# A GNN layer's block loop: the GRU job one step earlier, TensorE's block sums one step earlier, ScalarE's dense gates one step later

## What is computed

```
h = relu(layernorm(x))                              # x: 12500 nodes x 128
att = sigmoid(h[src] @ Wa[:128] + h[dst] @ Wa[128:] + b_att)   # 400000 edges
messages = (h[src] @ W_msg + b_msg) * att
agg = segment_sum(messages, dst)                    # real destinations: see below
r, z = sigmoid(gi_r + gh_r), sigmoid(gi_z + gh_z)   # gi = agg @ W_ih.T + b_ih
n = tanh(gi_n + r * gh_n)                           # gh = h @ W_hh.T + b_hh
out = x + batchnorm_over_nodes((1 - z) * n + z * h) * gamma + beta
```

## Time and profile before

| | |
|---|---|
| median of 3 runs | 2257.42 us (2254.52 to 2258.43) |
| the profiled execution | 2257.88 us |
| its span, first to last instruction | 2256.1 us |
| busy: PE, DVE, ACT, POOL | 91%, 89%, 88%, 74% |
| mean granted TensorE clock | 0.965 of full speed |

### The profile page before, as it was taken

One profiled execution on the slowest core, in us unless ns is written; L12 is line 12 of the kernel. 1 busy time (PEld: TensorE's weight loads), 2 busy tenths in 40 slices (PEclk: granted clock), 3 DMA queues, 4 the chain that ended last, 5 costly groups with the idle time before them and its releaser, 6 DMA issues.

```text
span 2256.1 us, 53903 instructions
## 1 busy us (share of the span) xinstructions
PE 2055.7 (91%) x18202; PEld 1994.3 (88%) x18202; DVE 2012.9 (89%) x4413; ACT 1996.3 (88%) x6980; POOL 1660.4 (74%) x1578
## 2 busy tenths in 40 slices
PE   3536999999999999999999999999999999999997
PEld 3525999999999999999999999999999999999996
DVE  5967899999999999999999999999999999999974
ACT  1368999999999999999999999999999999999943
POOL 4575777777777777777777777777777777777760
PEclk8865999999999999999999999999999999999998
DMA  6862222222222222222222222222222222222236
GB/s 164 237 172 62 56 60 62 59 60 60 62 62 62 63 58 64 61 63 59 63 59 62 59 61 60 63 60 62 60 61 63 59 62 60 61 61 64 58 108 231
DMA packets 167473, 171.57 MB, mean 76 GB/s; under 512 B 79462, under 2 KB 131736, under 8 KB 166944
## 3 DMA queue, kind: packets, MB, share of 16 engines
q0 software_dynamic: 49856, 102.96, 20.3%
q1 hardware_dynamic: 114564, 61.63, 10.5%
q10 hardware_dynamic: 2776, 3.52, 0.7%
HBM read 141.32 MB, written 26.65 MB: 74 GB/s over the span
## 4 chain that ended last, share of the span: by engine, by line
ACT 53%; PE 23%; DVE 14%; issue 7%; DMA 2%; SPq 1%; POOL 0%; ACTq 0%; DVEq 0%
ACT big L901 41%; PE ps L1456 12%; ACT gate_ring L897 9%; DVE big L1200 4%; PE ps L1441 4%; PE ps L1451 3%; DVE gate_ring L1184 2%; DVE key_hot L1170 1%; PE ps L1462 1%; PE ps L1463 1%; DVE lo_hot L1163 1%; DMA big<-in_x_dram 1%; DVE big L1129 1%; DMA row_ring<-node_table,set_idx 1%; ACT n_blk L906 1%
## 5 line engine op out<-in xcount | busy, mean ns | idle before, releaser
L773 POOL DMA_INDIRECT row_ring<-node_table,set_idx x1480 | 1571.8, 1062 | 473.4 <-issue 334.5
L901 ACT ACTIVATE big<-set_score,big 128x128 f32<-128x128 f32 x5096 | 1633.2, 394 | 81.0 <-PE ps L1456 80.7
L1456 PE MATMUL ps<-big 128*128 128x128 f32 x10192 | 1447.4, 281 | 0.0
L1456 PEld LDWEIGHTS ps<-big 128*128 128x128 f32 x10192 | 1265.0, 193 | 0.0
L1200 DVE TENSOR_TENSOR big<-ps,big 128x784 f32<-128x784 f32 x832 | 802.0, 964 | 10.2 <-ACT big L901 5.4
L1441 PE MATMUL ps<-gate_ring,row_ring 128*128 128x64 f32 x2960 | 534.8, 263 | 78.0 <-DVE gate_ring L1184 72.7
L1441 PEld LDWEIGHTS ps<-gate_ring,row_ring 128*128 128x128 f32 x2960 | 454.0, 194 | 124.4 <-DVE gate_ring L1184 110.7
L1184 DVE SCALAR_TENSOR_TENSOR gate_ring<-lane,set_rel,gate_ring 128x64 f32<-128x64 f32 x1480 | 412.9, 279 | 140.1 <-ACT gate_ring L897 135.0
L897 ACT ACTIVATE gate_ring<-set_win,row_ring 128x64 f32<-128x64 f32 x1480 | 493.2, 341 | 30.5 <-DMA row_ring<-node_table,set_idx 27.3
L1451 PE MATMUL ps<-key_hot,lo_hot 128*128 128x196 bf16 x3328 | 425.8, 250 | 14.4 <-DVE key_hot L1170 9.5
L1170 DVE TENSOR_TENSOR key_hot<-lane_key,set_key 128x1568 bf16<-128x1568 bf16 x416 | 402.0, 966 | 0.0
(11 more groups left out here) (129 smaller groups left out, 917.2 us busy)
## 6 DMA issues: line engine op xcount, KB each, us to landing
row_ring<-node_table,set_idx POOLq DMA_INDIRECT x1480
big<-in_x_dram SPq DMA_DIRECT2D x48, 256.0 KB, 5.6
h_blk<-hT_spill SPq DMA_DIRECT2D x97, 64.0 KB
node_table<-big SPq DMA_DIRECT2D x24, 258.0 KB
hT_spill<-big SPq DMA_DIRECT2D x24, 256.0 KB, 4.8
out_dram<-big SPq DMA_DIRECT2D x24, 256.0 KB
set_win<-dst_scores SPq DMA_DIRECT2D x148, 32.0 KB
set_score<-dst_scores SPq DMA_DIRECT2D x52, 64.0 KB
```

What stands on the lines that cost most here:

```text
L773: nc.gpsimd.indirect_dma_start(row_ring[:, t % ROWS_RING, :], None, table, bass.IndirectOffsetOnAxis(ap=set_idx[:, t // SET % 2, t % SET:t ...
L901: return nc.scalar.activation(a_buf[b % 2][:, h, :], set_score[:, b % 2, :], ACT.Sigmoid, bias=m_all[:, h, D:ROW])
L1456: return nc.tensor.matmul(ps[:, AM_BANK, 0:P], m_all[:, h, 0:D], a_buf[b % 2][:, h, :], start=h == 0, stop=h == HI - 1)
```

## The change

Three constants and one place in PE's order. The dense GRU job of a unit goes from step 2 to step 1 on PE. PE's 36 parts of block sums run in steps 2 to 37 in place of 3 to 38. ACT's 36 parts of dense gates run from step 8 to step 3 of the next unit in place of 7 to 2. In PE's step 2, where a `build` stands too, the block part now goes ahead of the `build`. The assertion is loosened to admit the new numbers. No instruction is added or removed.

```diff
-PARTS_AT = 3
-DENSE_AT = 7
+PARTS_AT = 2
+DENSE_AT = 8
 GROUP_LAG = 3
-GRU_AT = (2, 10, 18, 26, 33)
+GRU_AT = (1, 10, 18, 26, 33)
...
-                    if u < BLOCKS and s % PER_BEAT in (0, 2):
+                    builds = u < BLOCKS and s % PER_BEAT in (0, 2)
+                    if builds and s != PARTS_AT:
                         build(u, 2 * (s // PER_BEAT) + (s % PER_BEAT) // 2)
                     if u and s == PARTS_AT:
                         pe.wait_ge(pairs_kept, u * (2 * BEATS))
...
                         last.then_inc(block_parts, 1)
+                    if builds and s == PARTS_AT:
+                        build(u, 2 * (s // PER_BEAT) + (s % PER_BEAT) // 2)
                     k = job_at(u, s, GRU_AT)
```

More of the change, by code:

```diff
@@ L158, in gnn_program @@
     assert TILES % 2 == 1 and SPARSE < TILES and FINE <= P and GROWS <= P and HI <= P and 5 * GROWS <= 512 and KEYS <= 256
-    assert SPARSE % SET == 0 and GROUPS % 2 == 0 and DENSE_AT + PARTS < STEPS_U + 4 and PARTS_AT + PARTS < STEPS_U and SETS > 2 and TILES % 16 == 5
+    assert SPARSE % SET == 0 and GROUPS % 2 == 0 and DENSE_AT + PARTS <= STEPS_U + 4 and PARTS_AT + PARTS < STEPS_U and SETS > 2 and TILES % 16 == 5
     assert QCOLS == 2 * QHALF and (FINE + 1) * QHALF <= 512 and FINE * P <= QCOLS * P
```

## The result

The changed kernel took 2285.3 us (median of 4 runs, 2276.3 to 2287.9) against 2257.8 for the one before: 1.0108 of its time, 95% interval 1.0093 to 1.0122. It is slower by 27.5 us, outside the range of the prediction and on the other side of it. The interval leaves out 1, so the change makes it slower, though by little. The profiled execution has a span of 2286.2 us, 30.1 more than before.

A forecast was written before the change was run, and what follows sets the result against it. POOL, issuing gathers back to back at 38.6 us a unit and nearly level with the ACT-PE loop, was taken as the bound. 2257.9 - 5 - 0.6 - 7 = 2245 us, range 2216 to 2268, further down 2214 to 2266.

The forecast's parts named there:

- ACT's wait for PE goes: At ACT's first dense gate, 2.3 us of new slack against a 1.42 us wait: 80.7 us down to a few.
- POOL and the ACT-PE loop are bound nearly alike: Steady stretch: POOL's gathers take 38.6 us a unit, the whole length of a unit; ACT alone would need 37.0.
- POOL is slightly slower than the other engines already: Kernel before: POOL's lead in rows sinks and is never won back, so POOL sets when sparse tiles end.
- the sinking lead: Gathers started less gates started: 6 at 920 us, 3 at 1490, 5 at 2078; the ring would allow about 10.
- Point 1: First units, where POOL stands at the ring: the loop is 1.4 us a unit quicker in 4 units, -5 us.
- Point 2: After the last gather, PE has one part less to do behind the last scatter: -0.6 us.
- Point 3: POOL's gathers held under one-hot builds, 3.3 us a unit: 0.15 us a unit less for 46 units, -7 us.
- rival B: Builds and gathers fixed at a bad phase, one more gather a unit blocked by a `key_hots`: 2275 to 2282, chance 0.14.
- The GRU job's new place: PE's step 1: waits 0 to 0.3 us a unit for `keep_block`, beside 0.75 us idle time used up; taken as 0.
- the later last dense gates: `keep_pairs` in step 4 comes behind one more gate (0.24 us); taken as 0, at most 0.3 us a unit.
- Rival C: PE's clock falls to 1.2 GHz after waits, up to 0.2 us a unit, 2254; chance 0.25 together with no difference.
- Rival A: Full gain: POOL follows and a unit comes to ACT's 37.0 us, 2182 to 2195; chance 0.15 for 2215 or lower.

The follow-up runs named there:

- before_single: The kernel before with one-hot builds from unit 1 on replaced by DVE instructions with one SBUF input (dense-block counts left out): 2257.2 us against 2258.0, 0.9995.

## Why the prediction was wrong, point by point

The sum had three terms and a starting point. Taken in turn:

- "ACT's wait for PE goes": right, 80.7 us to 4.8, and its place was taken by waits for gathered rows, 27.3 to 76.2 us, as forecast.
- "POOL and the ACT-PE loop are bound nearly alike" was right as to their pace; "POOL is slightly slower than the other engines already" was wrong for the kernel before. 1245 gathers that fill 1700.8 us show that POOL did not wait, and not that others waited for it. ACT's waits for rows in the same stretch were 3.4 us, and I did not set them beside it; the 23.2 us of the earlier trace rows are of the last unit alone. before_single has POOL's work cut by 11% and the same time. I also read the sinking lead as POOL being the slower; it shows only that there was little spare.
- Point 1, 5 us from the ring in the first units: not seen. The waits of L773 for L1441 from 215 to 360 us are 13.8 us in 30 waits, against 16.4 in 34, 1.4 us less beyond the usual gap; the last gather started 30 us later all the same.
- Point 2, 0.6 us behind the last gather: right. From its start to the end of the span it is 63.6 us before and 63.0 now.
- The range was added up wrongly, too. Taken round the estimate of each, the bounds of points 1 and 3 give 2221 to 2273, not 2216 to 2268, and a second range (2214 to 2266) stands further down. The measured time is outside all three.
- Point 3 is the step that failed, by size and by sign: -0.15 us a unit was taken, and (1082 - 1061) x 28.27 = +0.59 was measured, somewhat over the 0.5 us that had been set as the bound. The ground given for the sign (builds that follow a landing fall well for the next gathers) was a guess. In the traces from 400 to 2100 us I count the gathers that are over 975 ns long and end 0.82 us after a build: behind a `key_hots` there are 225 against 183 before, 0.57 us late each in both; behind a `lo_hots` 102 against 108, 0.31 and 0.27 us late. The `key_hots` alone took 128.3 us from the gathers in place of 103.5, and that is all of the rise. It is one more gather held by a `key_hots` in each unit (42 in 44 units), the effect and the price (0.5 to 0.66 us) of rival B, which had a chance of 0.14 and gave 2275 to 2282. Why B came, a phase that is fixed at a bad point, is not shown.
- The part that had no term at all: what ACT does in step 8 behind the first dense gate. I followed PE's and DVE's moved steps and left out that ACT's waits for PE in step 7 had covered a second one, for L1225. It is 50.2 us in the changed kernel. It costs 29 us once the port is free. As the changed kernel stands, moving it away gave 15 us; whether by the wait itself or by where the builds then fall on the gathers is not shown.
- The GRU job's new place and the later last dense gates cost nothing, as taken: L1462's wait for L1206 is 0.5 us, L1200's for L901 5.3 us (5.4 before). Rival C did not come: PEclk is 0.970 over the span in place of 0.965. Rival A, a unit at 37.0 us, was not reached even with both obstacles gone (2208 in place of 2182 to 2195).

Shown: that the builds' hold on the gathers makes the changed kernel slower than it would be by 48 us, that it cost the kernel before under 10 us, and that the difference between the two lies in the length of the gathers, of those held by a `key_hots`. Not settled: why one more gather a unit is held by a `key_hots`. The end of a build fixes the start of the next gather behind it (end + 0.82 + 0.30), so builds and gathers can fall into a pattern, and the mean differs from kernel to kernel between 1061 and 1082 ns; I have no rule that gives it. Nor is it shown why POOL and the loop kept the same pace in the kernel before, where from 400 to 2100 us POOL never waited at the ring and ACT next to never for rows. A build with one operand in PSUM, which by L1200 would leave the gathers alone, was not tried.

## What to carry to other kernels

When a wait is removed from a loop that feeds on another engine's stream, look at what that stream does when it has to be on time: its average here was the same as the loop's to within a per cent, and its hidden delays (3.3 us a unit) cost next to nothing only as long as the loop had its own wait. An engine at 74% busy with equal small gaps has nothing to spare, but that doesn't say that it sets the pace. Read who waits for its product (ACT for rows: 3.4 us before, 43.0 after), and let one run with its disturbance taken away (here one operand fewer on DVE) confirm it before anything is built on it. And when an engine stops waiting at one place, walk its program on from there and ask of each later instruction what the old wait had hidden.

## What the runs showed of the hardware that was not expected

- A gather is held by DVE instructions with two SBUF operands, to 0.82 us after their end, and the short ones of the GRU job (0.28 us) do it too. One of 0.96 us with one operand in PSUM leaves it at 945 ns. With a sum over one operand in place of the builds (0.77 and 1.05 us) the gathers' mean was 945 to 951 ns, close to the shortest, 938 and 939. A `tensor_scalar` on bf16 with one SBUF tensor and a scalar column held those that started under it by a little: 989 ns in the mean.
- It is held through two builds back to back as through one (1.78 us, 0.82 after the second's end), so cutting them up does not help unless something else stands between.
- A `tensor_scalar` of 128 bf16 elements takes DVE 0.18 us in a row of eight, one of 196 elements 0.20: little of it is the elements.
- The same kernel took about 2258, 2567 and 2607 us on different chips; on the slower ones PE paused again and again, mostly for up to about 1 us, with nothing to wait for, and the mean granted clock was 0.93 to 0.95 in place of 0.963 to 0.970.
